# A GNN layer and an attention layer over a sparse graph: another order of SyncE's loads and writes, and a fourth adjacency buffer

## The chip, the cores and the metric

The kernel runs on one core of a Trainium2 chip. The metric is the device time of one execution in microseconds (us), less is better. A core has TensorE (PE), VectorE (DVE), ScalarE (ACT), GpSimd (POOL) and SyncE (SP), which run their own instruction streams and meet at semaphores, and 16 DMA engines. SyncE computes nothing here: it issues DMAs.

## The reference

Inputs are `x` (8192 x 256, float32) and `adj` (8192 x 8192, int32, 0 or 1, about two ones per row), and weights. Cut to what matters:

```python
h = relu(layernorm(x))
s = adj @ h[:, 0]                                   # zero where a row has no neighbour
x = x + relu(h @ w_self.T + s[:, None] * w_neigh.sum(axis=1)[None, :])
h = relu(layernorm(x))
Wh = (h @ W).reshape(8192, 4, 64)                   # 4 heads
sl, sr = (Wh * a_l).sum(-1), (Wh * a_r).sum(-1)
e = leaky_relu(sl[:, :, None] + sr.T[None, :, :], 0.2)    # only where adj + eye > 0
out = einsum('nhm,mhd->nhd', softmax(e), Wh)
x = x + elu(out)
```

Only the adjacency is large (268 MB); the attention needs each row's own entry and those of its few neighbours.

## The kernel before

The 8192 rows are worked in 64 tiles of 128 rows. `X` with all rows of x stays in SBUF. There are two stages that matter, with a short one between them.

**First stage, per tile.** SyncE loads the tile's adjacency in two halves of 128 x 4096 int32 (2 MB each) into a ring of `HALVES = 3` half-tile buffers `A` (function `load`, L254 to L260). The load number n goes to buffer n % 3; it waits until the semaphore `unloaded` shows that the half that lay there is packed (for the first three loads there is no wait). TensorE packs each half with 8 matmuls (`pack`, L676 to L687) into the bank `p_pack`, and raises `unloaded`. VectorE finds the neighbours of each row in it (`search`, `sort`), POOL gathers their first feature from a table in DRAM (L292), and TensorE, ScalarE and VectorE compute the layer's output and the table of rows for the attention, `row_table`, with 264 floats a row. The stages of one tile are spread over seven steps of the loop. Before it, the weights are prepared: their raw copies and `wa_tmp` lie in the upper part of `big`, behind the last buffer of the ring, and are last read by the set-up products of TensorE, ScalarE (`w_copied`, `vs_copied`) and VectorE (L348 to L354, semaphore `wa_step`, 8 in the end).

**Between the stages** tiles with too many neighbours would be listed for a separate dense path; with these inputs there are none.

**Second stage, per pair of tiles** (32 pairs, buffers in rings of `RING2 = 4`). Four things go on at once.

- SyncE runs `own_rows` (L885 to L891) and `write` (L893 to L897) in an order written out in L898. In step t it issues the load of pair t's own rows into `G[r]`, slot 0 (from the fifth pair on after a wait for `mixed` of pair t-4, which had the buffer), and then the write of the results of pair t-3, after a wait for `res_ready` of that pair. SyncE goes through these in order: what stands behind a wait stays there until it is met.
- POOL runs `gather` (L904 to L915): six indirect DMAs a pair from `row_table` into the other slots of `G[r]` and into `E[r]`, also after `mixed` of pair t-4.
- TensorE runs `scatter`, `spread` and `mix` (L920 to L955). The `mix` of a pair is 16 matmuls (L952 and L953), whose end raises `mixed`.
- VectorE runs a list of small steps for three pairs at once (L1099): `place` of pair t (L1012), which waits for the gathered rows and for the own rows, the scores of pair t, the weights of pair t-1 (L1053, L1060, L1071, L1075, L1081), and the results of pair t-3: `add_x` (L1090, after the write of the pair that had its buffer `res[r]`) and `take_low` (L1097), which raises `res_ready`. In the list `take_low` comes ahead of the second half of the scores of pair t.

Of the kernel before, what the change touches and what calls it, by code (L numbers as in the profile page):

```python
# [17 lines left out]
SLOPE = 0.2  # L18
RING = 3
RING2 = 4  # L20
HALVES = 3
SLOTS = 16
DIRECT = 2
EXTRA = SLOTS - DIRECT
# [10 lines left out]
def preln_gnn_gat_kernel(nc, x, adj, w_self, w_neigh, w_gat, a_l, a_r, out):  # L35
# [7 lines left out]
    HALF = N // 2  # L43
    DC = D // P
# [13 lines left out]
    THIRD, FULL = SLOTS, 2 * SLOTS  # L58
    MARKS = FULL + 2
    PAIRS = TILES // 2  # L60
    STAGING = (HALVES + 1) * HALF + 2560
    EMPTY = -0.5

    h0_dram = nc.dram_tensor("h0_table", [N, 1], F32, kind="Internal").ap()
# [3 lines left out]
    with ExitStack() as ctx:  # L68
        def sb(name, shape, dt=F32):
            return ctx.enter_context(nc.sbuf_tensor(name, shape, dt))  # L70
# [4 lines left out]
        def sem(name):  # L75
            return ctx.enter_context(nc.semaphore(name))
# [3 lines left out]

        big = sb("big", [P, STAGING], I32)

        A = [big[:, s * HALF:(s + 1) * HALF] for s in range(HALVES)]

        def low_bytes(b):
            return A[b].bitcast(F8)[:, 0:4 * HALF:4].rearrange("p (i o) -> p i o", o=WIDE)
# [4 lines left out]
        def of_big(*shape):  # L91

            width = int(np.prod(shape))
            used[0] += width
            part = bigf[:, used[0] - width:used[0]]
            if len(shape) == 1:
                return part
            if len(shape) == 2:
                return part.rearrange("p (a b) -> p a b", b=shape[1])
            return part.rearrange("p (a b c) -> p a b c", b=shape[1], c=shape[2])  # L100

        at = HALVES * HALF
        w_raw, wn_raw, wneighT = (bigf[:, at + i * DC * D:at + (i + 1) * DC * D].rearrange("p (c d) -> p c d", c=DC)
                                  for i in range(3))
        al_b, ar_b, wa_tmp = (bigf[:, at + (3 * DC + i) * D:at + (3 * DC + i + 1) * D] for i in range(3))
# [76 lines left out]
        w_in = sem("w_in")  # L182
        adj_in = [sem(f"adj_in{i}") for i in range(HALVES)]
        unloaded, pack_begun = sem("unloaded"), sem("pack_begun")
# [5 lines left out]
        w_turned, w_copied, wa_step = sem("w_turned"), sem("w_copied"), sem("wa_step")  # L190
        vs_done, vs_copied = sem("vs_done"), sem("vs_copied")
# [26 lines left out]
        def steps(depth, total):  # L218

            def num(k, r):  # L220

                return k * depth + r

            def later_round(k):

                return not isinstance(k, int) or k > 0

            def run(eng, *stages):


                def step(k, r):
                    for stage, lag in stages:
                        if not isinstance(k, int) or 0 <= num(k, r) - lag < total:
                            stage(k + (r - lag) // depth, (r - lag) % depth)
                for t in range(total + max(lag for _, lag in stages)):
                    step(t // depth, t % depth)
            return num, later_round, run
        num, later_round, run = steps(RING, TILES)
# [7 lines left out]
        with nc.Block() as block:  # L246

            @block.sync
            def _(sp):
                for c in range(TILES // XCH):  # L250
                    sp.dma_start(X[:, c * XCH:(c + 1) * XCH, :], x_tiles[:, c * XCH:(c + 1) * XCH, :]
                                 ).then_inc(x_in[c], 16)

                def load(k, r):  # L254
                    for s in range(2):
                        n = 2 * r + s
                        if later_round(k) or n >= HALVES:
                            sp.wait_ge(unloaded, num(k, r) * 2 + s + 1 - HALVES)
                        sp.dma_start(A[n % HALVES], adj[bass.ds(num(k, r) * P, P), s * HALF:(s + 1) * HALF]
                                     ).then_inc(adj_in[n % HALVES], 16)  # L260
                run(sp, (load, 0))
# [328 lines left out]
            def _(pe):  # L590
# [85 lines left out]
                def pack(k, r, s):  # L676
                        t = num(k, r)
                        if s == 0 and not (isinstance(t, int) and t == 0):
                            pe.wait_ge(searched, t)
                        n = 2 * r + s  # L680
                        pe.wait_ge(adj_in[n % HALVES], k * (2 * RING // HALVES * 16) + (n // HALVES + 1) * 16)
                        pe.sem_inc(pack_begun, 1)
                        for i in range(BLOCKS_IN // 2):
                            block_no = s * (BLOCKS_IN // 2) + i
                            last = nc.tensor.matmul(p_pack[:], pack_w[:, block_no, :], low_bytes(n % HALVES)[:, i, :],  # L685
                                                    start=(block_no == 0), stop=(block_no == BLOCKS_IN - 1))
                        last.then_inc(unloaded, 1)  # L687

                def pack_first(k, r):
                    pack(k, r, 0)  # L690

                def pack_second(k, r):
                    pack(k, r, 1)
# [147 lines left out]
        num, later_round, run = steps(RING2, PAIRS)  # L841
# [16 lines left out]
        res = [of_big(2, D) for _ in range(RING2)]  # L858
        assert used[0] <= STAGING
        p_ext, p_spread = p_hT, p_gT  # L860
# [20 lines left out]
        with nc.Block() as block:  # L881

            @block.sync
            def _(sp):
                def own_rows(k, r):  # L885
                    t = num(k, r)
                    if later_round(k):

                        sp.wait_ge(mixed, t - RING2 + 1)
                    sp.dma_start(G[r][:, :, 0, :], row_dram[bass.ds(t * (2 * P), 2 * P), :].rearrange("(a p) d -> p a d", p=P)  # L890
                                 ).then_inc(self_in[r], 16)  # L891

                def write(k, r):  # L893
                    t = num(k, r)
                    sp.wait_ge(res_ready, t + 1)
                    sp.dma_start(out[bass.ds(t * (2 * P), 2 * P), :].rearrange("(a p) d -> p a d", p=P), res[r]  # L896
                                 ).then_inc(pair_out[r], 16)  # L897
                run(sp, (own_rows, 0), (write, 3))  # L898
                for r in range(RING2):
                    sp.wait_ge(pair_out[r], 16 * len(range(r, PAIRS, RING2)))  # L900

# [373 lines left out]
```

## Time and profile before

| | us |
|---|---|
| three timed runs, median (lowest to highest) | 1049.7 (1049.09 to 1050.65) |
| the profiled execution's own time | 1043.53 |
| its span, from first to last instruction | 1041.7 |
| PE busy | 720.6 (69%) |
| DVE busy | 707.8 (68%) |
| POOL busy | 397.0 (38%) |
| ACT busy | 337.8 (32%) |
| 128 adjacency loads, 2048 KB each, median issue to landing | 12.8 |
| 32 own-row loads, 264 KB each, median issue to landing | 3.9 |
| 32 result writes, 256 KB each, median issue to landing | 2.2 |

The shares are averages over two unlike stages: the first stage lasts until about 737 us, the second from about 744 us to the end. A timeline or a chain has one row per group of instructions, with start and duration in us.

### The profile page before, as it was taken

How to read it: one execution, taken by the hardware profiler on the slowest of the kernel's cores; microseconds unless marked ns; L12 is line 12 of the kernel's file. 1: busy time of each engine (PE TensorE's matmuls, PEld its weight loads, DVE VectorE, ACT ScalarE, POOL GpSimd, SP SyncE). 2: the span in 40 equal slices, each digit the busy share in tenths (PEclk: the TensorE clock that was granted, in tenths of full speed). 3: DMA queues.
4: the chain of work that ended last, by engine and by line, in shares of the span. 5: the costliest groups of instructions: out<-in, count | busy, mean ns of one | idle time of the engine just before them, and what ended most of it. 6: DMA issues, size and time to landing. Idle time of an engine off the chain costs nothing. (4 is left out here: it accounts for less than half of the span.)

```text
span 1041.7 us, 13552 instructions
## 1 busy us (share of the span) xinstructions
PE 720.6 (69%) x3025; PEld 478.0 (46%) x3026; DVE 707.8 (68%) x2868; ACT 337.8 (32%) x1481; POOL 397.0 (38%) x458
## 2 busy tenths in 40 slices
PE   1366877877787778687877787786256766766674
PEld 1134544545444444354445444454145555655564
DVE  6656676776677766766676677675257777777776
ACT  1023333333434343434343343335122222232222
POOL 0032323232323232322323232322277767767660
PEclk9988887888888887988788888888577897789879
DMA  9999999999999999999999999990224444444442
GB/s 305 381 423 416 423 422 422 415 420 419 415 408 417 406 408 409 408 417 402 417 407 408 404 409 406 423 385 23 79 70 131 129 120 127 125 126 130 123 122 63
DMA packets 70000, 321.94 MB, mean 309 GB/s; under 512 B 14498, under 2 KB 48721, under 8 KB 53536
## 3 DMA queue, kind: packets, MB, share of 16 engines
q1 hardware_dynamic: 44160, 293.88, 69.9%
q0 software_dynamic: 15360, 17.46, 7.2%
q10 hardware_dynamic: 10400, 9.74, 2.8%
q8 instruction: 26, 0.43, 0.2%
q14 instruction: 54, 0.44, 0.1%
HBM read 312.57 MB, written 17.07 MB: 316 GB/s over the span
## 5 line engine op out<-in xcount | busy, mean ns | idle before, releaser
L685 PE MATMUL p_pack<-big,pack_w 128*128 128x512 fp8e5 x1024 | 316.9, 462 | 150.8 <-DMA big<-in_adj_dram 139.5
L292 POOL DMA_INDIRECT h0g<-h_table,nbr x192 | 191.6, 998 | 476.1 <-ACT nbr L527 390.8
L685 PEld LDWEIGHTS p_pack<-big,pack_w 128*128 128x128 fp8e5 x1024 | 105.4, 108 | 301.2 <-issue 224.3
L912 POOL DMA_INDIRECT big<-row_table,lists x192 | 196.6, 1024 | 97.1 <-issue 54.1
L361 DVE MAX8 tops<-p_pack 128x8 f32<-128x256 f32 x128 | 48.9, 423 | 157.6 <-PE p_pack L685 157.6
L952 PE MATMUL p_u<-big,ident 128*128 128x256 f32 x288 | 94.9, 478 | 62.1 <-DVE big L1081 62.1
L491 ACT ACTIVATE nbr<-keys 128x2 uint32<-128x2 f32 x64 | 13.0, 203 | 366.3 <-DVE keys L396 366.3
L952 PEld LDWEIGHTS p_u<-big,ident 128*128 128x128 f32 x288 | 67.2, 241 | 77.3 <-DVE big L1081 65.3
L650 PE MATMUL p_u<-wselfT,hT 128*128 128x256 f32 x256 | 82.0, 453 | 0.0
L672 PE MATMUL p_row<-w_gat_and_heads,gT 128*128 128x264 f32 x256 | 69.7, 396 | 0.6 <-ACT rows L580 0.6
L650 PEld LDWEIGHTS p_u<-wselfT,hT 128*128 128x128 f32 x256 | 57.6, 249 | 6.5
L1012 DVE TENSOR_TENSOR big<-onehot_all,big 128x112 f32<-128x112 f32 x32 | 8.8, 275 | 76.2 <-DMA big<-row_table 56.6
L1060 DVE TENSOR_TENSOR big<-big,p_pack 128x768 f32<-128x768 f32 x64 | 58.2, 950 | 1.1
L564 ACT ACTIVATE g<-x_rows,nm,rs 128x256 f32<-128x256 f32 x64 | 38.4, 600 | 60.3 <-DVE nm L462 59.8
L365 DVE FIND_INDEX8 found<-tops,p_pack 128x8 uint32<-128x256 f32 x128 | 52.6, 423 | 0.0
L626 PEld LDWEIGHTS p_u<-beyond,mapT 128*128 128x128 f32 x128 | 36.7, 287 | 23.7 <-issue 14.6
L672 PEld LDWEIGHTS p_row<-w_gat_and_heads,gT 128*128 128x128 f32 x256 | 44.7, 195 | 5.6 <-issue 1.2
L952 PE MATMUL p_row<-big,ident 128*128 128x256 f32 x96 | 32.1, 484 | 20.9 <-DVE big L1081 20.9
L977 ACT ACTIVATE big<-big 128x136 f32<-128x136 f32 x32 | 10.1, 316 | 109.8 <-DVE big L1039 109.8
L986 ACT ACTIVATE big<-p_u 128x512 f32<-128x512 f32 x24 | 14.3, 597 | 78.8 <-PE p_u L953 78.8
L535 ACT ACTIVATE h<-x_rows,nmr,rstd 128x256 f32<-128x256 f32 x64 | 37.4, 585 | 0.0
L619 PEld LDWEIGHTS p_u<-extra_all,earlier 128*128 128x128 f32 x128 | 21.6, 190 | 32.0 <-DVE picked L419 26.8
(146 smaller groups left out, 1369.8 us busy)
## 6 DMA issues: line engine op xcount, KB each, us to landing
big<-in_adj_dram SPq DMA_DIRECT2D x128, 2048.0 KB, 12.8
row_table<-rows ACTq DMA_DIRECT2D x64, 132.0 KB, 9.6
big<-row_table SPq DMA_DIRECT2D x32, 264.0 KB, 3.9
x_rows<-in_x_dram SPq DMA_DIRECT2D x8, 1024.0 KB, 12.6
out_dram<-big SPq DMA_DIRECT2D x32, 256.0 KB, 2.2
h0g<-h_table,nbr POOLq DMA_INDIRECT x192, 6.2
big<-row_table,lists POOLq DMA_INDIRECT x192, 2.8
big<-in_L_gnn_w_self_dram ACTq DMA_DIRECT2D x1, 256.0 KB, 4.9
```

What stands on the lines that cost most here:

```text
L292: nc.gpsimd.indirect_dma_start(out=h0g[r][:, j:j + 1], out_offset=None, in_=h0_dram[:, :], in_offset=bass.IndirectOffsetOnAxis(ap=nbr[r][: ...
L361: nc.vector.max(tops[r][:, 8 * half:8 * half + 8], p_pack[:, half * WIN:(half + 1) * WIN]).then_inc(search_step, 1)
L365: last = nc.vector.max_index(found[r][:, 8 * half:8 * half + 8], tops[r][:, 8 * half:8 * half + 8], p_pack[:, half * WIN:(half + 1) * WIN])
L535: nc.scalar.activation(h[r][:], x_tile(k, r), ACT.Relu, bias=nmr0[:, bass.ds(t, 1)], scale=rstd0[:, bass.ds(t, 1)]).then_inc(h_ready, 1)
L564: nc.scalar.activation(g[r][:], x_tile(k, r), ACT.Relu, bias=nm1[r][:], scale=rs1[r][:]).then_inc(g_ready, 1)
L626: nc.tensor.matmul(p_edge[:, 0:EXTRA + 1], mapT[r][:], beyond[r][:], start=True, stop=True).then_inc(spread_ready, 1)
L650: nc.tensor.matmul(p_first[:, 0:D], hT[r][:, c * P:(c + 1) * P], wselfT[:, c, :], start=(c == 0), stop=(c == DC - 1))
L672: last = nc.tensor.matmul(p_row[:, 0:ROW], gT[r][:, c * P:(c + 1) * P], wx[:, c, :], start=(c == 0), stop=(c == DC - 1))
L685: last = nc.tensor.matmul(p_pack[:], pack_w[:, block_no, :], low_bytes(n % HALVES)[:, i, :], start=(block_no == 0), stop=(block_no == BLOC ...
L912: nc.gpsimd.indirect_dma_start(out=dst, out_offset=None, in_=row_dram[:, :], in_offset=bass.IndirectOffsetOnAxis(ap=lists[r][:, a, j:j + 1 ...
L952: nc.tensor.matmul(part, ident[:], G[r][:, a, j, 0:D], start=(j == 0), stop=False)
L1060: nc.vector.tensor_tensor(rows_by_head, rows_by_head, w, ALU.mult).then_inc(weighed, 1)
```

## The change

The ring of half-tile buffers gets a fourth buffer. It lies where the weights' raw copies were, which stay at the same address, so that they and the fourth buffer share the place; the whole of `big` keeps its size. The load that first uses that buffer, number 3, waits for the set-up work that reads the raw copies. The wait counts are now computed from the running number of the half. In the second stage the write that SyncE issues in step t is that of pair t-5 instead of t-3.

```diff
-HALVES = 3
+HALVES = 4
...
-    STAGING = (HALVES + 1) * HALF + 2560
+    STAGING = HALVES * HALF + 2560
...
-        at = HALVES * HALF
+        at = (HALVES - 1) * HALF
...
                 def load(k, r):
                     for s in range(2):
-                        n = 2 * r + s
-                        if later_round(k) or n >= HALVES:
-                            sp.wait_ge(unloaded, num(k, r) * 2 + s + 1 - HALVES)
+                        n = 2 * num(k, r) + s
+                        if n >= HALVES:
+                            sp.wait_ge(unloaded, n + 1 - HALVES)
+                        elif n == HALVES - 1:
+
+                            sp.wait_ge(vs_copied, 1)
+                            sp.wait_ge(w_copied, 2)
+                            sp.wait_ge(wa_step, 4 * DC)
                         sp.dma_start(A[n % HALVES], adj[bass.ds(num(k, r) * P, P), s * HALF:(s + 1) * HALF]
                                      ).then_inc(adj_in[n % HALVES], 16)
...
-                        n = 2 * r + s
-                        pe.wait_ge(adj_in[n % HALVES], k * (2 * RING // HALVES * 16) + (n // HALVES + 1) * 16)
+                        n = 2 * t + s
+                        pe.wait_ge(adj_in[n % HALVES], (n // HALVES + 1) * 16)
...
-                run(sp, (own_rows, 0), (write, 3))
+                run(sp, (own_rows, 0), (write, 5))
```

## Rows read from the trace of the kernel before

**Rows 1.** The page, 40 equal slices: busy tenths of the DMA engines, GB/s.

```profile
DMA  9999999999999999999999999990224444444442
GB/s 305 381 423 416 423 422 422 415 420 419 415 408 417 406 408 409 408 417 402 417 407 408 404 409 406 423 385 23 79 70 131 129 120 127 125 126 130 123 122 63
```

**Rows 2.** Windows: length, busy us (count) by engine, PE clock, DMA share, GB/s.

```profile
60.00:700.00 640.00, 491.62 (x2098) 296.85 (x2099) 440.53 (x2045) 242.44 (x1204) 189.49 (x244) 0.84 1.01 413
787.50:1019.40 231.90, 158.53 (x652) 132.74 (x651) 171.65 (x487) 60.10 (x158) 164.03 (x161) 0.84 0.46 126
```

**Rows 3.** Waits of the whole run: waiting instruction, releaser, total us, times, longest.

```profile
PE p_pack L685 <- DMA big<-in_adj_dram: 139.5, 65, 3.9
...
DVE big L1012 <- DMA big<-row_table: 56.6, 27, 2.8
```

**Rows 4.** The chain of waits that ended last, one piece: start, us, what.

```profile
844.80 3.80 DMA big<-row_table
```

**Rows 5.** Timeline of SyncE: one result write and the own-row load behind it.

```profile
844.37 0.38 SPq L896 DMA_DIRECT2D out_dram<-big  x1
844.80 0.47 SPq L890 DMA_DIRECT2D big<-row_table  x1
```

**Rows 6.** Timeline of VectorE: `place` (L1012) of four pairs, and one L1097.

```profile
787.51 0.28 DVE L1012 TENSOR_TENSOR big<-onehot_all,big 128x112 f32<-128x112 f32 x1 [2.29 <-DMA big<-row_table,lists]
...
840.22 0.28 DVE L1012 TENSOR_TENSOR big<-onehot_all,big 128x112 f32<-128x112 f32 x1 [2.19 <-DMA big<-row_table]
...
843.66 0.68 DVE L1097 TENSOR_TENSOR big<-big 128x512 f32<-128x512 f32 x1
...
848.72 0.28 DVE L1012 TENSOR_TENSOR big<-onehot_all,big 128x112 f32<-128x112 f32 x1 [2.10 <-DMA big<-row_table]
...
1019.39 0.28 DVE L1012 TENSOR_TENSOR big<-onehot_all,big 128x112 f32<-128x112 f32 x1 [1.40 <-DMA big<-row_table]
```

**Rows 7.** Windows at the start of the first stage.

```profile
44.00:46.00 2.00, 2.00 (x7) 0.62 (x5) 0.00 (x0) 0.00 (x0) 0.00 (x0) 1.00 0.49 205
46.00:48.00 2.00, 2.00 (x8) 0.67 (x6) 0.00 (x0) 0.00 (x0) 0.10 (x1) 1.00 0.71 156
```

**Rows 8.** Timeline at the start: end of the set-up, and the fourth adjacency load.

```profile
41.53 0.42 DVE L350 TENSOR_REDUCE w_gat_and_heads<-big 128x4 f32<-128x256 f32 x1
...
45.76 0.33 SPq L259 DMA_DIRECT2D big<-in_adj_dram  x1
```

**Rows 9.** Timeline of TensorE: first and last matmuls of three mixes, start of a fourth.

```profile
846.04 2.93 PE L952 MATMUL p_u<-big,ident 128*128 128x256 f32 x6 [3.44 <-DVE big L1081]
...
850.77 0.59 PE L953 MATMUL p_u<-big 128*128 128x256 f32 x2
...
854.54 1.56 PE L952 MATMUL p_u<-big,ident 128*128 128x256 f32 x6 [2.34 <-DVE big L1081]
...
857.66 0.59 PE L953 MATMUL p_u<-big 128*128 128x256 f32 x2
...
880.67 2.93 PE L952 MATMUL p_u<-big,ident 128*128 128x256 f32 x6 [2.32 <-DVE big L1081]
...
886.81 0.64 PE L953 MATMUL p_u<-big 128*128 128x256 f32 x2
...
889.91 2.59 PE L952 MATMUL p_u<-big,ident 128*128 128x256 f32 x6 [1.63 <-DVE big L1081]
```

**Rows 10.** Groups by line from 787.5 to 1019.4 us: busy, mean ns, idle before, releasers.

```profile
L912 POOL DMA_INDIRECT big<-row_table,lists x161 | 164.8, 1024 | 64.1 <-issue 44.9 <-PE p_u L953 12.1 <-PE p_row L953 7.2
...
L1012 DVE TENSOR_TENSOR big<-onehot_all,big 128x112 f32<-128x112 f32 x28 | 7.7, 275 | 58.9 <-DMA big<-row_table 56.6 <-DMA big<-row_table,lists 2.3
```

**Rows 11.** Timeline of POOL: three gathers, in brackets the idle time before.

```profile
784.12 1.00 POOL L912 DMA_INDIRECT big<-row_table,lists  x1 [0.30 <-issue]
...
843.80 1.42 POOL L912 DMA_INDIRECT big<-row_table,lists  x1 [0.30 <-issue]
...
852.23 1.49 POOL L912 DMA_INDIRECT big<-row_table,lists  x1 [1.80 <-PE p_u L953]
```

## The prediction

> **What bounds the kernel now.** I read the page's slices first. The DMA engines are full in the first 27 of 40 slices and under half full in the other 13 [rows 1], so there are two kernels in one. The stage windows give the numbers: from 60 to 700 us the DMA share is 1.01 at 413 GB/s, with every compute engine partly idle; from 787.5 to 1019.4 us it is 0.46, and there no engine is full: POOL 164.0 and DVE 171.7 of 231.9 us [rows 2]. The list of waits says what is late in each. In the first stage TensorE's packing waits for adjacency, 139.5 us in 65 waits; in the second VectorE waits 56.6 us in 27 waits for the own rows (big<-row_table, the load by SyncE), and not for the gathered ones [rows 3]. The chain of waits, once in each turn of the loop, goes through the landing of such a load, here 3.80 us [rows 4]. SyncE's timeline shows why the load is late: it goes out 0.43 us after the result write of the same step, which had waited for L1097 [rows 5]. VectorE's timeline gives the turn: `place` of one pair at 840.22, L1097 ends at 844.34, the load starts at 844.80, the next `place` is at 848.72 [rows 6]. From pair 4 (787.51) to pair 31 (1019.39) that is 27 turns in 231.9 us, 8.59 us each.
>
> **Part 1: the fourth half-tile buffer.** What decides is whether DMA time is ever unused. In the long stretch it isn't (share 1.01), so there the extra transfer in flight only queues longer: 0 us. The exception is the start. From 44 to 46 us the share is 0.49, from 46 to 48 us 0.71 [rows 7], because the fourth load is issued at 45.76, after the first packing has emptied a buffer; its new wait is on set-up work whose last instruction, L350, ends at 41.95 [rows 8]. The other two conditions are products of the set-up that come earlier. So the load starts some 3.8 us earlier and fills the hole. Idle time in the hole: 2 x 0.51 + 2 x 0.29 = 1.6 us. By bytes: (413 - 205) x 2 + (413 - 156) x 2 = 930 KB, at 413 GB/s 2.3 us. I take 2.0 us. As the stage is full of DMA afterwards, everything behind shifts by it. The further loads wait for one unload less; SyncE has nothing else in that block, so nothing is queued behind them. Bounds: 0 below (the hole filled by nothing), and above, should the deeper queue also lift the rate, see rival B. The other edits of this part (wait counts, addresses of the staging area, same total size) cost nothing: as many instructions as before on each engine, and SyncE's and TensorE's new wait values stand for the same kind of waits.
>
> **Part 2: SyncE's order.** In step t SyncE now issues the own rows of pair t, behind a wait for the mix of pair t-4, and then the write of pair t-5 instead of t-3. Nothing is added, and no DMA is dropped. The own rows of pair t+1 thus pass the writes of t-4 and t-3. They wait for the mix of t-3, which ends in turn t-1 at the latest (the mix that began in the turn of the `place` at 840.22 ended at 851.36, 11.1 us after it [rows 6, 9]); the rows are wanted at turn t+1, more than a turn later, so their 3.8 us are hidden. The write of pair t-5 stands behind the wait for the mix of t-4. That mix ends 11.1 us after `place` of t-3, so 3.1 us into turn t-2 at a turn of 8 us, while L1097 of pair t-5 ends 4.1 us into the same turn: the write leaves when it did before. Should a mix be slower, the write is late by 1 or 2 us, and its buffer is wanted three turns later. Queued behind SyncE's last writes is only the end of the block. Cost 0.
>
> Then what is late next? VectorE without that wait needs (231.9 - 58.9) / 27 = 6.41 us a turn. POOL needs more: its 161 gathers in the stretch are busy 1.024 us each, and between two of them lies the issue gap of 0.30 [rows 10, 11]. Six per pair: 6 x (1.024 + 0.304) = 7.97 us. Without any lengthened gather it would be 6 x 1.30 = 7.80. POOL's real waits, for a mix to free a buffer, are all that keeps it at 8.59 now: 12.1 + 7.2 us in the stretch, less 15 ordinary gaps in them, 14.8 us.
>
> Does the mix free the buffers in time at 7.97? The last gather of a pair starts 3.39 us before `place` (784.12 to 787.51 [rows 6, 11]), the first five pitches of 1.33 earlier, so 10.0 us before. For the pair three turns on, that is 23.9 - 10.0 = 13.9 us after a `place`. The mix is done at 11.1 us and POOL starts 0.87 later (851.36 to 852.23), 12.0 in all: 1.9 us to spare. But TensorE has two speeds here (granted clock 0.84 on average [rows 2], a mix of levels 2.4 and 1.2 GHz): the mix at 880.67 took 6.8 us, the one at 846.04 took 5.3 us, and the shortest wait between the end of one and the start of the next is 2.5 us (887.45 to 889.91, scatter, spread, and VectorE's L1071 to L1081) [rows 9]. TensorE's own loop is therefore 5.3 + 2.5 = 7.8 us in the usual case and 9.3 in the slow one. A slow mix makes a turn late by up to 1.3 us; the spare time, 0.4 us for such a mix, covers part. Four of the 27 mixes of the stretch are over 6 us, like this one; each costs between 0 and 1.3 us, I take 0.75, so 3 us.
>
> Sum: 27 x 7.97 + 3 = 218.2 us instead of 231.9, 13.7 us less. Turns 0 to 3 are POOL's already (pair 4 still waited for gathered rows at 787.51), and the 22 us after pair 31 hold no own-row load: both unchanged. Bounds: 27 x 7.80 = 210.6, 21.3 us less; and if TensorE's loop sets half of the turns, rival A.
>
> A rule bears on POOL's 1.024. The row: VectorE's L1097 ran from 843.66 to 844.34, and the gather that began at 843.80 took 1.42 us instead of 1.00 [rows 6, 11]. The Trainium skill ("SBUF — State Buffer", the section on which ports are shared) says that a VectorE instruction with two SBUF inputs and a GpSimd one that reads SBUF share a read port, held for a whole instruction; the trace agrees, with 0.42 us for 0.54 us of overlap left. With POOL pacing, the two would lock in phase and the rule would hit one gather per pair by about 0.25 us, 8.05 us a turn and 2 us less gain than the mean that I use.
>
> The profiled execution took 1043.5 us (span 1041.7), 6.2 below the median of 1049.7. Its own sum: 1043.5 - 2.0 - 13.7 = 1027.8; shifted by the same 6.2, the predicted median is 1034.0 us.
>
> **Rivals.**
> A. TensorE paces instead of POOL. For it: 7.8 us of loop against POOL's 7.97, and a clock that wavers. Against: a mix at the full clock takes 3.7 us (the one at 854.54 [rows 9]), and its loop 6.2. If usual (5.3) and slow (6.8) mixes alternated, a turn would be 6.05 + 2.46 = 8.5 us, and the second stage would give 2.4 us: 1045; with half of that effect 1040.
> B. The deeper ring also lifts the first stage's rate, since a DMA engine that is ahead of the others has one more load to begin. For it: the rate is 413 on the mean and 420 to 423 in six of the page's slices [rows 1]. Against: a share of 1.01. At 420 GB/s the 640 us would become 629: 1023.
> C. Slower. Gathers on POOL are lengthened by VectorE's two-input instructions (the row above) so that POOL's turn passes 8.59: that takes 0.79 us a pair over the free pace of 7.80, two full hits of 0.49. With 1.0 us a pair the stage takes 27 x 8.8 = 237.6, 5.7 us more, less 2.0 at the start: 1053. For it: each gather is open to it. Against: now it is 0.16 us a pair, and L1097 is the only such instruction over 0.3 us in a turn.
> D. The order doesn't free the own rows, as some wait in SyncE's queue holds them until L1097 all the same: 2.0 us at the start alone, 1047.7. Against: both waits ahead are met in an earlier turn.
>
> **How the numbers follow.** Forecast 0.68 (its own range 1029 to 1039: the bounds of both terms), A 0.13, B 0.12, C 0.03, D 0.04. Between 1025 and 1042 us lie the forecast and the nearer half of A and B, which leaves about 0.19 outside. What this kernel's measurement can tell from no change is about 0.2%, 2.1 us. Faster by more: forecast, A and B, 0.93; within it D, 0.04; slower C, 0.03.
>
> **What would show it.** Right: no VectorE wait for big<-row_table by SyncE; instead short waits for the gathered rows at `place`, turns of about 8.0 us, POOL idle only for issue gaps; at the start a share near 1 from 44 to 48 us; the first stage 2 us shorter at the same GB/s. Wrong: PE as releaser of POOL or of VectorE's L1021 and L1071 in most turns (A), over 416 GB/s from 60 to 700 us (B), a mean gather over 1.15 us (C), own-row loads that still follow L1097 (D).

## The result and the profile after

The changed kernel takes 1026.3 us (median of three runs, 1024.5 to 1027.2) against 1049.7 us: ratio 0.977, 95% interval 0.975 to 0.980, so 23 us less by the medians, 21 to 26 by the interval. Two more comparisons on other occasions gave 0.979 (0.976 to 0.982) and 0.981 (0.978 to 0.983); all three together say 20 to 24 us. The forecast was 1034.0 us, a gain of 15.7. The spans of the two traces are 1041.7 and 1024.5 us, 17.2 us apart.

The windows of the page after, with those of the two stages (columns as in [rows 2]; the second window runs from `place` of pair 4 to `place` of pair 31):

```profile
60.00:690.00 630.00, 467.11 (x2079) 279.49 (x2078) 436.05 (x2032) 239.10 (x1188) 186.53 (x240) 0.88 1.01 416
785.50:1000.90 215.40, 151.20 (x640) 127.59 (x639) 172.46 (x486) 59.28 (x156) 164.44 (x161) 0.84 0.50 134
```

Against [rows 2] the same POOL work, 164 us, now stands in 215.4 us instead of 231.9: 7.98 us a turn. VectorE's own-row wait [rows 3, 10] is gone, and in its place it waits for the gathered rows. The groups by line of that stretch, columns as in [rows 10]:

```profile
L917 POOL DMA_INDIRECT big<-row_table,lists x161 | 164.9, 1024 | 49.0 <-issue 47.5 <-PE p_u L958 0.9 <-PE p_row L958 0.6
L1017 DVE TENSOR_TENSOR big<-onehot_all,big 128x112 f32<-128x112 f32 x27 | 7.5, 276 | 37.1 <-DMA big<-row_table,lists 37.1
```

POOL's idle time before a gather is nothing but issue gaps: the 19.3 us put down to TensorE in [rows 10] are 1.5 us, and those are five ordinary gaps of 0.30. VectorE still has 37.1 / 27 = 1.4 us a turn to spare. The timeline of SyncE and VectorE shows a turn (start, duration):

```profile
834.15 0.30 DVE L1017 TENSOR_TENSOR big<-onehot_all,big 128x112 f32<-128x112 f32 x1 [0.48 <-DMA big<-row_table,lists]
...
837.63 0.68 DVE L1102 TENSOR_TENSOR big<-big 128x512 f32<-128x512 f32 x1
...
838.50 0.37 SPq L895 DMA_DIRECT2D big<-row_table  x1
838.92 0.47 SPq L901 DMA_DIRECT2D out_dram<-big  x1
...
841.86 0.28 DVE L1017 TENSOR_TENSOR big<-onehot_all,big 128x112 f32<-128x112 f32 x1 [0.34 <-DMA big<-row_table,lists]
...
849.29 0.28 DVE L1017 TENSOR_TENSOR big<-onehot_all,big 128x112 f32<-128x112 f32 x1 [1.03 <-DMA big<-row_table,lists]
```

The load still goes out near the end of the subtraction (L1097 before, L1102 now), but it does not wait for it: it goes 0.03 us after the mix that frees its buffer (last matmul L958, 837.88 to 838.47). It is ahead of the write, and it fetches the rows of a pair two places further on: they are for the `place` at 849.29, not for that at 841.86. And the hole of [rows 7] is filled:

```profile
44.00:46.00 2.00, 2.00 (x6) 0.74 (x5) 0.00 (x0) 0.00 (x0) 0.00 (x0) 1.00 1.03 422
46.00:48.00 2.00, 2.00 (x6) 0.74 (x5) 0.00 (x0) 0.00 (x0) 0.10 (x1) 1.00 1.00 427
```

### The profile page after: what moved, and what is told of

The parts are those of the page before. It is cut to its first block and busy times, and to the rows that moved or that the text cites. A ratio compares the mean times of both kernels' runs of the same rounds, so it can differ in the third digit from the quotient of the medians.

```text
span 1024.5 us, 13553 instructions
## 1 busy us (share of the span) xinstructions
PE 701.5 (68%) x3025; PEld 464.3 (45%) x3026; DVE 709.2 (69%) x2868; ACT 337.7 (33%) x1481; POOL 397.3 (39%) x458
## 5 line engine op out<-in xcount | busy, mean ns | idle before, releaser
L690 PE MATMUL p_pack<-big,pack_w 128*128 128x512 fp8e5 x1024 | 305.9, 450 | 165.6 <-DMA big<-in_adj_dram 148.8
L690 PEld LDWEIGHTS p_pack<-big,pack_w 128*128 128x128 fp8e5 x1024 | 102.9, 106 | 313.7 <-issue 234.6
L655 PE MATMUL p_u<-wselfT,hT 128*128 128x256 f32 x256 | 77.9, 434 | 0.0
L655 PEld LDWEIGHTS p_u<-wselfT,hT 128*128 128x128 f32 x256 | 53.7, 233 | 5.9
L631 PEld LDWEIGHTS p_u<-beyond,mapT 128*128 128x128 f32 x128 | 33.4, 262 | 21.2 <-issue 11.5
```

The costliest lines, as they stand in the source:

```text
L631: nc.tensor.matmul(p_edge[:, 0:EXTRA + 1], mapT[r][:], beyond[r][:], start=True, stop=True).then_inc(spread_ready, 1)
L655: nc.tensor.matmul(p_first[:, 0:D], hT[r][:, c * P:(c + 1) * P], wselfT[:, c, :], start=(c == 0), stop=(c == DC - 1))
```

## The experiments

Three comparisons, each with its own runs of the kernel before. Every kernel left a trace too; the places read from them are in the table at the end of the section.

**The two parts alone**, and the changed kernel beside them.

> The changed kernel as it is, on the same chip as its parts. By the traces the change is worth 17 us (spans 1041.7 and 1024.5), by the medians 23.4. If the profiled execution of before was a quick one of its kind, the difference here is again 20 us or more; if the two sets of runs differed by chance, it is 17.

Measured: 1025.0 us against 1045.8, ratio 0.979 (0.976 to 0.982). The gain by medians is 20.8 us here, over the 20 us that were to speak for a quick trace of before.

```diff
 kernel before
-                run(sp, (own_rows, 0), (write, 3))
+                run(sp, (own_rows, 0), (write, 5))
```

> Ring of three as before, SyncE's write five pairs behind. Theory (POOL's six gathers a pair pace the second stage): turns of 7.98 us from pair 4 to pair 31, 15 to 16.5 us less than before, first stage unchanged. Rival (the ring brought part of the second stage's gain too): under 12 us less.

Measured: 1029.0 us, ratio 0.983 (0.981 to 0.986): 17.6 us less by the ratio, 16.7 by the medians, where 15 to 16.5 were expected. Turns of 8.04 us. The order alone does all that happens in the second stage, with no help of the ring.

```diff
 changed kernel
-                run(sp, (own_rows, 0), (write, 5))
+                run(sp, (own_rows, 0), (write, 3))
```

> Ring of four, SyncE's order as before. Theory (the ring only fills the hole in DMA time at the start): 1.6 to 2.4 us less than before, the same GB/s from 60 to 690 us. Rival (the deeper ring also helps the steady part of the first stage, in timed runs more than in the profiled one): 6 to 9 us less than before in the medians.

Measured: 1043.1 us, ratio 0.996 (0.994 to 0.998), 2 to 6 us less, 4.1 by the ratio and 2.7 by the medians. That is between the two theories. The GB/s from 60 to 690 us did rise, to 417, against 413 in [rows 2]; the theory said it would not.

```diff
 changed kernel
                         elif n == HALVES - 1:
+                            sp.wait_ge(unloaded, 1)
```

> The changed kernel, but the fourth adjacency load waits for the first packing as it did before, so that the hole at 44 to 48 us comes back while the ring stays four deep. Theory (hole only): 1.6 to 2.4 us slower than the changed kernel, so the same time as with the order alone. Rival (depth of the ring matters in the steady part): within 1 us of the changed kernel, or at least 4 us faster than the order alone.

Measured: 1025.7 us, ratio 0.981 (0.979 to 0.984). By the ratio that is between the changed kernel (0.979) and the order alone (0.983); by the medians it is 0.7 us above the one and 3.4 below the other, nearer the rival. So it was run again.

**Other sizes of each part.**

```diff
 changed kernel
-                run(sp, (own_rows, 0), (write, 5))
+                run(sp, (own_rows, 0), (write, 4))
```

> The changed kernel with the write four pairs behind the own rows instead of five. Theory: what counts is that the own-row load of pair t+1 does not stand behind the L1097 of turn t; with four it stands behind that of turn t-1, a whole turn of 8 us earlier, and 3 to 4 us of landing fit in. The same time as the changed kernel, within 2 us, and no wait of VectorE for the own rows. Rival (own rows and writes on one queue disturb one another): 3 us or more slower than the changed kernel.

Measured: 1025.3 us, ratio 0.980 (0.975 to 0.984), turns of 7.96 us, no wait for own rows. So one place less is enough. SyncE's timeline of this kernel has the load behind the write again, as in [rows 5], and it does no harm, since the load is a turn early:

```profile
838.84 0.38 SPq L901 DMA_DIRECT2D out_dram<-big  x1
839.27 0.47 SPq L895 DMA_DIRECT2D big<-row_table  x1
```

```diff
 changed kernel
+                    sp.dma_start(E[r][:, 1, :], row_dram[bass.ds(t * (2 * P), P), :]).then_inc(self_in[r], 16)
...
                         for j in range(OWN):
+                            if a == 1 and j == DIRECT:
+                                continue
```

> The changed kernel with five instead of six gathers a pair on POOL; the sixth (second tile's extra rows) is replaced by a plain load of as many rows by SyncE, of the wrong rows, so that part of the attention is computed with other data. Theory (POOL paces): POOL's turn falls from 7.98 to 6.64 us and something else paces, VectorE at 6.41 or TensorE's loop at 6.2 to 7.8 by its clock: turns of 6.7 to 7.5 us, with the first four pairs 20 to 36 us less than the changed kernel. Rival A (TensorE's loop of 7.8 us paces, or nearly): turns above 7.7 us, 7 to 12 us less.

Measured: 991.2 us, 34 us less than the 1025.3 us of the kernel above; that one stands for the changed kernel in this comparison. Turns of 6.94 us. Windows and groups by line of its second stage:

```profile
780.00:967.60 187.60, 134.77 (x651) 116.84 (x650) 172.89 (x487) 60.30 (x160) 134.10 (x133) 0.93 0.58 163
```

```profile
L920 POOL DMA_INDIRECT big<-row_table,lists x133 | 134.1, 1008 | 50.9 <-issue 38.4 <-PE p_u L961 9.2 <-PE p_row L961 3.3
L1020 DVE TENSOR_TENSOR big<-onehot_all,big 128x112 f32<-128x112 f32 x28 | 7.6, 272 | 1.0 <-DMA big<-row_table,lists 0.5 <-issue 0.2
```

VectorE is busy 172.9 of 187.6 us and no longer waits for rows (1.0 us in 28 places), and POOL waits for buffers again. So VectorE paces now, or nearly: of the 14.7 us that it is idle, 6.5 are waits for TensorE's `scatter` by the list of waits. TensorE's loop, 7.8 us in the usual case by rival A, let turns of 6.94 pass, at a granted clock of 0.93 on average: here 21 of the 27 mixes took 3.7 us and none over 6, where the trace after has 12 and 5.

```diff
 changed kernel
                             dst = E[r][:, a, :] if j == DIRECT else G[r][:, a, j + 1, :]
+                            if a == 1 and j == DIRECT:
+                                nc.gpsimd.indirect_dma_start(
+                                    out=spare[r][:], out_offset=None, in_=row_dram[:, :],
+                                    in_offset=bass.IndirectOffsetOnAxis(ap=lists[r][:, a, j:j + 1], axis=0),
+                                    bounds_check=N - 1, oob_is_err=False).then_inc(rows_in[r], 16)
```

> The changed kernel with a seventh gather a pair, the second tile's extra rows once more into a spare buffer; the result is the same. Theory (POOL paces): each gather is worth its pitch of 1.33 us in every pair, turns of 9.30 us, 41 to 44 us more than the changed kernel. Rival A (TensorE paces at 7.8): up to 0.2 us a pair less, 35 to 38 us more.

Measured: 1066.6 us, 41.3 more than the 1025.3 beside it. Turns of 9.35 us, where 7 x 1.33 is 9.3: each gather has its full price. The windows of the stretch show POOL busy 193.7 of 252.5 us, the rest its issue gaps:

```profile
790.60:1043.10 252.50, 169.81 (x650) 139.74 (x649) 170.80 (x487) 60.09 (x158) 193.68 (x188) 0.80 0.45 122
```

```diff
 changed kernel
                         elif n == HALVES - 1:
+                            sp.wait_ge(unloaded, 3)
```

> The changed kernel with the fourth adjacency load held back until three halves are packed, so that no load is under way from about 45 to 54 us. Theory (DMA bytes pace the first stage from the start to the last load, and DMA time lost at the start is lost at the end): 8 to 9.5 us more than the changed kernel, first place some 9 us later. Rival (the engines that compute pace part of the stage and a ring of four makes good what is lost): under 6 us more.

Measured: 1034.8 us, 9.5 more than the 1025.3 beside it, and the first `place` at 762.30, 8.5 us after 753.8, the mean of the seven traces with the hole filled. The windows show the widened hole:

```profile
46.00:48.00 2.00, 2.00 (x9) 0.63 (x6) 0.00 (x0) 0.00 (x0) 0.10 (x1) 1.00 0.08 33
48.00:50.00 2.00, 0.20 (x1) 0.00 (x0) 1.66 (x6) 0.00 (x0) 0.00 (x0) 1.00 0.00 0
```

From 44 to 56 us the share leaves 7.7 us of idle DMA time. DMA time lost at 45 us is lost at 750: the transfers pace the first stage up to the last load, and a ring of four makes nothing good.

**More runs, for the sizes.**

> The kernel before as it is, for a second trace of it and for what one kernel differs from itself. Theory (the forecast's 13.7 us for the second stage was low partly because the profiled execution of before was a quick one): turns from pair 4 to pair 31 of 8.65 us or more, against 8.59 in the first trace. Rival: 8.59 again or less, and the whole of the difference lies in the turns after.

Measured: ratio 1.000 (0.998 to 1.002), turns of 8.66 us in its trace (span 1048.6 us).

> The order alone once more, to tell it from the changed kernel with more runs. Theory: 1.5 to 3 us slower than the changed kernel, first place at 755 to 756 us. Rival (the ring is worth 4 us or more in the first stage): over 4 us slower.

Measured: 1030.2 us, ratio 0.984 (0.981 to 0.986). It is 3.3 us above the changed kernel by medians and 3.2 by ratios, between the theory's bound of 3 and the rival's of 4; by the ratios of the first try the difference was 4.5, so 3.9 over both. The first `place` was at 758.5, later than was expected, as it was in the trace of the kernel before taken beside it (758.4).

> Ring of four with the hole at the start left in, once more, since the first try lay between the two theories. Theory (hole only): the time of the order alone. Rival (depth helps in the steady part): the time of the changed kernel or less.

Measured: 1029.2 us, ratio 0.982 (0.980 to 0.985).

> The changed kernel once more, beside the order alone and the late fourth load. Theory: 1.5 to 3 us faster than either; rival (depth): as fast as the late fourth load and over 3 us faster than the order alone.

Measured: 1026.9 us, ratio 0.981 (0.978 to 0.983), 3.3 us faster than the order alone and 2.2 faster than the late fourth load. Neither theory's picture: the late load lies between the two, and so it does over both tries (mean ratios 0.980, 0.982, 0.983).

The table has the starts of `place` in the traces, us (two values: two traces, three: three):

| kernel | `place`, pair 0 | turns 4 to 31, mean | from `place` of pair 31 to the end |
|---|---|---|---|
| before | 755.4, 758.4 | 8.59, 8.66 | 22.3, 24.2 |
| ring only | 753.6 | 8.72 | 23.3 |
| order only | 755.7, 758.5 | 8.04, 7.98 | 23.0, 22.3 |
| late fourth load | 753.9, 756.9 | 7.94, 7.99 | 23.1, 23.7 |
| changed | 753.8, 756.0, 752.2 | 7.98, 8.03, 7.98 | 23.6, 22.8, 23.2 |
| lag of four | 754.3 | 7.96 | 25.4 |
| wide hole | 762.3 | 8.06 | 22.3 |
| five gathers | 752.9 | 6.94 | 24.3 |
| seven gathers | 754.0 | 9.35 | 22.3 |

None of these versions with the full result beats the changed kernel; with the lag of four, which had no run of the changed kernel beside it, it is the same within what can be measured.

## Why the prediction was right, and where its sizes were off

**What bounds.** Right in both stages. Own rows behind L1097 were what was late in the second stage: with them out of the way the turn fell from 8.6 to 8.0 us. Transfers pace the first stage: a wider hole came out in full.

**Part 2, mechanism.** Right: no wait for own rows, POOL idle for issue gaps alone. The term 6 x (1.024 + 0.304) = 7.97 us a turn was exact: 7.94 to 8.04 in seven traces of this order with the hole as it was or filled. The turn even follows the mean gather of its own trace: 7.94 us where that is 1.018 us (late fourth load), 8.04 where it is 1.037 (order only). The 8.05 that the prediction set beside its mean, a lock in phase with VectorE's two-input instructions, is reached in such a trace and is not the rule: in the trace after the mean gather is 1.024 us, as before. Six, five and seven gathers confirm that POOL paces at six and above, and that at five VectorE takes over, or nearly.

**Part 2, the 3 us for slow mixes: wrong.** This term was mis-sized: it came to next to nothing. 27 x 7.97 is 215.2 us, and the seven traces have 215.8 on the mean, 0.6 more. The slow mixes are still there: five of 27 took over 6 us in the trace after, four in that of before. The timeline of TensorE in the trace after, first and last matmuls of one that took 6.4 us, and the `place` of VectorE that fell into it:

```profile
824.25 2.93 PE L957 MATMUL p_row<-big,ident 128*128 128x256 f32 x6 [3.42 <-DVE big L1086]
...
830.03 0.59 PE L958 MATMUL p_row<-big 128*128 128x256 f32 x2
```

```profile
825.67 0.28 DVE L1017 TENSOR_TENSOR big<-onehot_all,big 128x112 f32<-128x112 f32 x1 [0.84 <-DMA big<-row_table,lists]
```

That turn took 8.48 us (to 834.15), the next two 7.71 and 7.43: 7.87 on the mean. I had charged a late turn to the total, as if what paces were on the same chain. But POOL paces, and its gathers went on meanwhile, since the buffers were free in time: the forecast had 0.4 us to spare for a slow mix, this one ended at 830.62 and POOL's first gather into its buffers began at 831.55, with an issue gap alone before it. VectorE does come late, but out of its 1.4 us of slack a turn: its wait at `place` falls to 0.48 and 0.34 us and is back at 1.03. In the whole stretch it never falls to nothing, so even the turn of 8.48 us was ended by gathered rows and not by the mix: POOL's last gathers of the two pairs began at 822.19 and 830.25, 8.06 us apart, and the other 0.42 us is that the rows took longer to land. A late turn of VectorE costs something only from the point at which its slack is used up or POOL has to wait.

**Part 2, the size of before.** The trace of before on which the sum stands was a quick one of its kind: 8.59 us a turn, where the two other traces with SyncE's old order have 8.66 and 8.72. Against their mean, 233.7 us for the 27 turns, the gain is 17.9 us. The forecast took one profiled execution, 6.2 us under the median of the runs, and carried the difference of 6.2 over to the kernel after unchanged; some 2 us of it lay in these turns. Pairs 0 to 4 gave 0.6 us more (32.2 us from first to fifth `place` with the old order, 31.6 with the new one), which I had at nothing. The cause is open. Pair 4's own rows, too, stood behind a write, and with the lag of four, where they do so again, it is 32.2 us; but with the old order and the new one alike the `place` of pair 4 waited for gathered rows (2.29 us in [rows 6], 1.94 in the trace after).

**Part 1: right in kind, short in size.** 2.0 us were forecast; by the starts of pair 0 the ring gives 3.2 us (757.0 on the mean of four traces with three buffers, 753.8 on that of seven with four). Half of it is the hole: with the late fourth load the mean is 755.4. The other half, 1.6 us, would be the depth in the steady part, which the forecast had at 0. The timed runs divide it alike: mean ratios of 0.980, 0.982 and 0.983 for the changed kernel, the late fourth load and the order alone. Traces of one kernel differ by 3 to 4 us in that place, and the intervals of the ratios are about 2.4 us to either side, so the half that goes to depth is not settled by these runs; that the hole counts is shown by the wide hole.

**Rival B: the rate rose, and its gain did not come.** The forecast said that over 416 GB/s from 60 to 700 us would show a faster first stage. In that window the trace after has 413, as before; but its last part holds no load any more. From 60 to 690 us all nine traces with a ring of four and a hole no wider than before have 415 to 417, the four with three buffers 412 or 413. Four GB/s more over 630 us would be 6 us; yet what depth may have given is 1.6. The windows at the end of the stage, before and then after, say why:

```profile
695.00:700.00 5.00, 4.80 (x18) 3.01 (x19) 2.87 (x12) 1.25 (x5) 2.83 (x4) 0.66 1.00 393
700.00:705.00 5.00, 3.58 (x19) 2.01 (x17) 4.35 (x24) 2.67 (x15) 0.16 (x1) 1.00 0.34 125
```

```profile
690.00:695.00 5.00, 2.90 (x10) 1.01 (x9) 3.56 (x14) 3.76 (x19) 1.97 (x3) 0.81 0.89 353
695.00:700.00 5.00, 5.00 (x26) 3.48 (x25) 3.06 (x15) 0.00 (x0) 1.15 (x2) 0.85 0.08 28
700.00:702.00 2.00, 1.42 (x7) 0.56 (x5) 1.82 (x11) 1.53 (x11) 0.00 (x0) 1.00 0.06 26
```

After, the DMA engines are nearly done at 695 us: a share of 0.08 is little more than one engine of 16. But TensorE's last packing still waits for its half (timeline of TensorE, after):

```profile
704.17 2.29 PE L690 MATMUL p_pack<-big,pack_w 128*128 128x512 fp8e5 x5 [2.42 <-DMA big<-in_adj_dram]
```

The share of 0.06 is one engine of 16, and 26 GB/s are a sixteenth of 416. The packets in the trace show the same: from 694.9 to 702.6 us those of the adjacency loads follow one another singly, 16 KB and 0.611 us each, never two at a time. Of the sixteen increments with which the last load raises its semaphore, fifteen are there by 694.67 and the last comes at 702.93; only then does TensorE's wait end, at 704.17. In the four traces with three buffers an engine is alone for the last 3.4 to 4.0 us of the loads (4 or 5 packets), in the ten with four buffers for 6.7 to 9.9 us (9 to 14). A load is 8 packets for each engine, so the others have run up to a load further ahead. That is also what the rate shows: four GB/s over 630 us are 2.5 MB, a little more than one load. It raises the mean GB/s and ends in fifteen engines standing idle. That it is the same engine from the start, which sets the pace with either ring, is inferred; the trace does not name it, and no run here made its share smaller. The Trainium skill ("DMA: Bandwidth & Descriptors", section "Latency and other measured facts") says that two of the sixteen, 7 and 15, are usually slower in traces. One slow engine agrees with that, without showing its number; the page ties the slowness, as a guess, to DMAs that GpSimd issues, and these loads are SyncE's.

**Rivals A, C, D.** A is refuted by the trace after, where POOL has no wait for TensorE beyond ordinary gaps. Its 7.8 us took a mix of 5.3 us as the usual one; but ten of the 27 mixes of before took 3.7 us, and the mean was 4.95, in the trace after 4.80, so with 2.46 us between mixes the loop is at 7.3. Five gathers let turns of 6.94 us pass, though at a higher clock. C did not come: POOL's mean gather is 1.024 us as before, and 1.037 at most with this order. D is refuted by the order alone.

**The sum.** 17.9 + 0.6 + 3.2 = 21.7 us by the traces, 20 to 24 by the timed runs; the forecast had 13.7 + 0 + 2.0. The 6.0 us between are 2.4 of slow mixes, 1.8 of a quick trace of before, 0.6 of the first pairs and 1.2 of the ring.

The median of 1026.3 us is 7.7 under the forecast of 1034.0. The 1.7 us beyond these 6.0 lie in the comparison: its 1049.7 for the kernel before is 2.6 to 4.4 above the medians of the three later ones (1047.1, 1045.8, 1045.3). So 1026.3 is outside the forecast's own range, 1029 to 1039. It is within 1025 to 1042 only because the lower end of that was set to take in the nearer half of rival B, whose gain did not come; that it lies inside is to that extent luck.

## What to carry to other kernels

An in-order queue that only issues DMAs can still be the bound: look at what each load stands behind, and issue it when its buffer is free and not when some result is ready; one turn earlier was enough here. When the wait is gone, the next bound is the sum of busy time and issue gaps of the engine that repeats the same work (here POOL: six gathers of 1.33 us), and jitter of the others costs nothing as long as that one never waits. A mean GB/s over a stage can rise without the stage's end moving, so read the windows behind the last load too.

## What the hardware showed that I had not expected

- A mean DMA share of 1.01 hides that one of 16 engines is behind: the share fell from 0.89 to 0.08 within 10 us, and TensorE still waited for a load until 704 us.
- POOL's indirect DMA of 128 rows costs its engine 1.00 us and a gap of 0.30, lengthened now and then (1.42 us in [rows 11], 1.02 on the mean): 7.98 us a pair with six, 9.35 with seven.
- TensorE's granted clock rose with the pace: 0.80 on average at 9.35 us a turn, 0.84 to 0.87 at 7.94 to 8.06, 0.93 at 6.94. Less idle time between mixes went with a higher clock, so the loop that was feared as a bound was quicker: a mix took 4.80 us on the mean at turns of 7.98 and 4.05 at 6.94.
